# Score products over 64 rows instead of 32, other loads for their operands, and a new merge order

## Chip, cores and metric

One Trainium2 chip, one of its cores. The time is the device time of one execution in microseconds (us); lower is better. The kernel before takes 1289.83 us in the median of three runs.

## What is computed

The input `x` is 8 batches of 512 tokens by 128 features. Two blocks follow each other, both with a residual that is scaled by a gate per batch:

```python
h = layernorm(x) * (1 + ca) + sa
x = x + ga * global_attention(h)     # 16 heads of 8 channels over all 512 positions
h = layernorm(x) * (1 + cb) + sb
x = x + gb * local_attention_ffn(h)  # 2 layers: 8 heads of 64, windows of 64 tokens, then a gated MLP
```

The global attention, called A here, projects q, k and v (128 by 128 weights), regards them as 16 heads, and computes for each head

```python
attn = softmax(einsum('bhdt,bhds->bhts', k, v) * temperature)   # 512 x 512 for each of 16 heads
out  = einsum('bhdt,bhts->bhds', q, attn)
```

The contraction of the scores runs over only 8 channels. Each of k and v is split into a rounded high part and a low rest, and the four products of the parts are summed inside one matmul: 4 x 8 = 32 rows of contraction for a head.

## The kernel before

**Three streams.** For each engine the work is written as generators: stream `a` is the global attention of all 8 batches, stream `x` the local layers of the batches 0, 1, 2, 4, 6, stream `y` those of the batches 3, 5, 7. `merge` advances the generators in the order that a string names, one string per engine (`ORDER`, lines 65 to 117), one letter for a step. All engines execute their instructions in that fixed order and wait for each other by semaphores. `BANKS` (lines 118 to 130) gives the PSUM bank of every TensorE result in its order. Stream `y` shares memory with A, so it starts when A is through. So there are two phases: A with part of `x`, then `x` with `y`.

**Steps of A.** A batch has 16 groups (a group is 4 heads, one in each quarter q of the channels, at one quarter j of the 512 positions t), each group 2 steps (`half`) of 2 heads. A step: TensorE makes a pair of score products (`a_scores`, L436, 128 x 512 each, into two neighbouring banks); VectorE takes the maximum over both (`a_max`, L1151); ScalarE makes two exponentials with row sums (`a_exp`, L866). After two steps VectorE inverts the four sums, GpSimd scales q by them (L764), and TensorE adds the product with q for four heads (`a_values`, L445). The score pairs run two steps ahead of the exponentials. The next batch is prepared within the steps of the one before (normalization, transposition, projections, splitting into parts on GpSimd at L747 and L749).

**The path of k and v.** The parts go to DRAM (`k_scr`, `v_scr`, shape 4 quarters q x 4 heads hh x 4 parts x 8 channels x 512; L656) and come back as rows of 32 for a head: `v_rows` (two slots, for even and odd batches) and `k_rows` (one slot). A head of quarter q lies at 32 rows that rotate with hh, so a load for one hh takes one DMA of 4 quarters or two DMAs of 3 + 1, 2 + 2 or 1 + 3 quarters (`PIECES`, `rows_in`, L362): 7 DMAs for k and 7 for v in each batch. SP issues v first (`a_values_in`), then k for hh = 0 to 3 (`a_keys_in`), where the k of a hh waits until the batch before has used that slot; for batch 0 the v loads are issued by ScalarE. `a_scores` waits for v and k of its hh at the first step of each hh.

Of the kernel before, what the change touches and what calls it, by code (L numbers as in the profile page):

```python
# [48 lines left out]
PIECES = [[(q, n, (q + hh) % HQ) for q, n in ((0, HQ - hh), (HQ - hh, hh)) if n] for hh in range(HQ)]  # L49
# [44 lines left out]
    "ACT": (
        "aaaaaaaaaaaaaaaaaaaaaaaaaaaaaaaaaaaaaaaaaaaaaaaaaaxaaaaaaaaaaaaxxaaaxaaaxxaxxaaxxxaaxxxaxaaxaaaxxxxa"
        "xxxaaaxxaaaxaaxaaxaxxxxxaxxxaxxxaaaaaxaaxaaaaaxaaaaxaaxaaaxaaxaaxaxxaaxxxxxxxxxaxaaaxxxaxxaaaxaxaaax"
        "xaaaaaaxxaxaxaxxxaxxxxaaxxxaxaxaaaaaxaaaxaaaaaaaxaaaxaaaaaaaaaaaaaxaaaxaaxaxaxxxaxxaxxxaxxaxaxaaxxax"
        "xaaaxxaxxxaaaxxaxxxxaaaaxaaxxxaxaaxxaaxaaaaxxaaaaaxaaaaxaaaaxaaxaaaaaaaxaaaaaaaaaxxxxxxaaxxaxxxaxxxx"
        "xxaaxxxaxxaaaxxaxaaxxxxxaxxxaxxxaaxxaaaaaaaxaaaaxaaaaaaxxyyyxyyyxxyyyxxxxxxxxxxxxyyxyxxxxyyxxyxxxyxx"
        "xxxxyxxyyxxxyxyxxyyyyxxyyyxyyyyxyyxyyxyyyxyxxxxxxxxxxxxyxxxxyxxxxxyxxyxxxxxyxxxxxxxxyxxyyyxyyyyxyyxy"  # L100
        "yxyyyyyyyyxyyyxxyyxxyyyyyxxyxyyxyyxyxxxyxyyxxxxyxxxxxyxxxyxxxxxyxxxxxxxxxxyyxyyyxyyyyyyyxyyyxyyyyyxy"
        "yyxyyxxxxyxxyxxyxxxyyyxyyyyxxxyxyyxyxyxxyxxxyxxxxyxxyxxxxyxxyxxyyyyxyyyyxyyyxyxyyyyyyyyyyxyxxyxyxxyy"
        "xyyxyyxyxyyxxyxxyxxyyxxxxyxxxxyxxyxxxxxxxxxyxxxxxxyyxyyxyyyyyyxyyyyyxyyyyyxyyyxyyxyyyxxxxyyyxyyxyyyx"
        "yyyxxxyyxxxyxxxyxxxxyxyxxyxxxyxyyyyyyyyyyyxyyyyyxyxxyxyyyxxyyyyyyxyyxyyyyyyxyyxxyxyyy"
    ),
    "POOL": (
        "aaaaaaaaaaaaaaaaaaaaaaaaaaaaaaaaaxaxaxxaxaxxxxxaxxxaxxxaaaaxxaaxxxaxxaaaxaaaaaaaaaaaaxxxxxxxxxxaxxaa"
        "xxaxxaaaaaaxxaxaxxxaxaxaaaaaaaaaaaaaaaaaaaaaaxxxaxxxxxaxxxxaxxxaaxaaaxaxxaxaaxxaxxaaaaaaaaaaaaaaaaaa"
        "aaxxxaxaxxxxxxxxxxxxaaaaxxaxxxaxxaxaaaaaaaaaaayyyxxxxxxxxxxxxxxxxyyyyyyxxyxyxyyxyxyyxxyyyyyyyyxxxxxx"
        "xxxxxxxxxxxxxxxxxxyyyyyyyyyyyyyyyyyyxyyyxxyyxyxxxxxxxxxxxxxxxxxxxxyyyyyyyyyyyyyyyyxxxyxyxyxxyxxyxxyx"  # L110
        "xyxxyxxxxxxxxxyyyyyyyyyyyyyyyyyyxyxyyxyxyxyxxxxxxxxxxxxxxxxxxxyyyyyyyyyyyyyyyyxyyyxxyxyyyxyxxxxxxxxx"
        "xxxxxxyyyyyyyyyyyyxyyyyxxxyyyyyyyy"
    ),
    "SP": (
        "aaaaaaaaaaaaaaxaaaaaaaaaxaaaaaaaaaaaxaaxaaaaaaaaaaaaaxxxyxxyxyyxxyxyyxyxy"
# [22 lines left out]
def build(nc, x, wmod, wqkv1, wqkv, wo, w1, w2, cols_in, rows_in_, rotary, out):  # L138
    with ExitStack() as ctx:
# [503 lines left out]
        def _(sp):  # L643
# [776 lines left out]
```

## Time and profile before

| | |
|---|---|
| median of 3 runs | 1289.83 us (1284.92 to 1290.12) |
| the profiled execution | 1282.93 us, of which its span (first to last instruction) 1280.9 us |
| TensorE busy in the span | 1047.0 us (82%) |
| VectorE | 957.4 us (75%) |
| ScalarE | 920.6 us (72%) |
| GpSimd | 505.4 us (39%) |
| mean granted TensorE clock | 0.909 of full |

Engines: PE is TensorE's matmul, PEld its weight load, DVE VectorE, ACT ScalarE, POOL GpSimd, SP the engine that issues most DMAs. "Granted clock" is 1.00 for 2.4 GHz and 0.50 for 1.2 GHz, or a mean of the two over a stretch. A bracket with an arrow at the end of a timeline row is the idle time of the engine before the instruction and what ended it.

### The profile page before, as it was taken

Reading aid. Unit: us, or ns where it says so; the run is one execution under the profiler, and the core shown is the slowest. Engines: PE = TensorE matmul, PEld = TensorE weight load, DVE = VectorE, ACT = ScalarE, POOL = GpSimd, SP = SyncE. Lnnn points to the kernel's source line nnn. Section 1 sums busy time; section 2 is a strip of 40 time slices with the busy share of each in tenths; the row PEclk is TensorE's granted clock in tenths of the full one; section 3 lists DMA queues with packets and bytes.
Section 4 is the critical chain, followed back from the end, with each engine's and each line's share of the span. In section 5 each row is a group of like instructions: output and inputs, shape, how many; then the busy total and the mean of one; then the engine's idle time right before and its main releaser. Section 6 shows DMA issues by size and latency. Waiting matters only on the chain. (4 is left out here: it accounts for less than half of the span.)

```text
span 1280.9 us, 23838 instructions
## 1 busy us (share of the span) xinstructions
PE 1047.0 (82%) x8124; PEld 521.6 (41%) x8124; DVE 957.4 (75%) x1945; ACT 920.6 (72%) x2782; POOL 505.4 (39%) x577
## 2 busy tenths in 40 slices
PE   2677978788887888888887888898888987888887
PEld 1232334233432343234234545455355445445463
DVE  2669887788788979886788585885884777687745
ACT  1687969678997799969856757577577666676684
POOL 4111244033310631153039363564374356266550
PEclk7687869798996899879898999899999999999989
DMA  6331212103121040301001101011011011010010
GB/s 209 144 124 48 86 43 68 66 1 109 53 71 70 1 138 25 99 34 31 1 8 30 30 1 30 9 30 30 9 31 30 1 38 30 9 30 18 14 31 17
DMA packets 24647, 59.15 MB, mean 46 GB/s; under 512 B 2832, under 2 KB 3024, under 8 KB 23376
## 3 DMA queue, kind: packets, MB, share of 16 engines
q1 hardware_dynamic: 23394, 55.53, 14.4%
q10 hardware_dynamic: 1134, 2.10, 0.5%
q8 instruction: 67, 1.10, 0.4%
q14 instruction: 52, 0.43, 0.1%
HBM read 23.98 MB, written 18.87 MB: 33 GB/s over the span
## 5 line engine op out<-in xcount | busy, mean ns | idle before, releaser
L866 ACT ACTIVATE E<-psum,neg_max 128x512 f32<-128x512 f32 x512 | 347.9, 718 | 80.3 <-DVE neg_max L1151 56.5
L1151 DVE TENSOR_REDUCE neg_max<-psum 128x2 f32<-128x1024 f32 x256 | 307.8, 1214 | 75.3 <-PE psum L436 73.3
L786 POOL TENSOR_TENSOR work<-work,rot_work 128x512 f32<-128x512 f32 x128 | 162.6, 1271 | 154.2 <-DVE rot_work L1218 152.3
L436 PE MATMUL psum<-v_rows,k_rows 32*128 32x512 f32 x512 | 133.8, 557 | 100.9 <-ACT E L866 47.3
L799 POOL TENSOR_TENSOR rot_work<-rot_work,rz 128x512 f32<-128x512 f32 x128 | 132.8, 1039 | 206.3 <-DVE rz L1245 206.2
L960 ACT ACTIVATE rot_work<-psum,neg 128x128 f32<-128x128 f32 x512 | 184.5, 407 | 34.1 <-DVE neg L1240 26.2
L494 PE MATMUL psum<-wqkv_sb,hs 128*128 128x512 f32 x384 | 191.1, 633 | 7.3 <-DVE hs L1208 4.4
L764 POOL TENSOR_TENSOR qz<-qT,rz 128x32 f32<-128x32 f32 x128 | 30.8, 241 | 337.1 <-DVE rz L1155 337.0
L445 PE MATMUL psum<-E,qz 128*32 128x512 f32 x1024 | 162.2, 711 | 0.0
L436 PEld LDWEIGHTS psum<-v_rows,k_rows 32*128 32x128 f32 x512 | 52.9, 205 | 247.4 <-issue 122.3
L794 POOL TENSOR_TENSOR work<-work,rn 128x512 f32<-128x512 f32 x128 | 133.1, 1053 | 16.8 <-DVE rn L1110 16.6
L960 ACT ACTIVATION_READ_ACCUMULATOR rot_work<-psum,neg 128x1 f32 x512 | 124.6, 248 | 0.0
L866 ACT ACTIVATION_READ_ACCUMULATOR E<-psum,neg_max 128x1 f32 x512 | 121.7, 238 | 0.0
L501 PE MATMUL psum<-ident,work 128*128 128x128 f32 x512 | 88.8, 311 | 37.1 <-POOL work L794 22.8
L932 ACT ACTIVATE rot_work<-psum 128x512 f32<-128x512 f32 x128 | 76.9, 604 | 58.1 <-DVE ss L1222 35.2
L1240 DVE TENSOR_REDUCE neg<-psum 128x4 f32<-128x512 f32 x128 | 85.6, 678 | 40.2 <-PE psum L519 39.8
L494 PEld LDWEIGHTS psum<-wqkv_sb,hs 128*128 128x128 f32 x384 | 67.7, 197 | 93.4 <-issue 47.9
L1214 DVE TENSOR_TENSOR work<-psum,rot 128x512 f32<-128x512 f32 x128 | 87.2, 681 | 20.9 <-ACT rot_work L932 20.7
L569 PE MATMUL psum<-work,w_sb 128*128 128x512 f32 (+1 forms) x192 | 93.3, 610 | 11.4 <-ACT work L975 7.8
L529 PE MATMUL psum<-ident,rot_work 128*128 128x128 f32 x512 | 82.4, 287 | 22.5 <-POOL rot_work L799 12.5
L501 PEld LDWEIGHTS psum<-ident,work 128*128 128x128 f32 x512 | 63.5, 157 | 79.1 <-POOL work L794 53.8
L970 ACT ACTIVATE prT<-psum 128x512 f32<-128x512 f32 x128 | 81.1, 646 | 15.3 <-PE psum L540 12.3
(121 smaller groups left out, 1679.0 us busy)
## 6 DMA issues: line engine op xcount, KB each, us to landing
work<-v_al SPq DMA_DIRECT2D x16, 512.0 KB, 4.4
work<-v_al SPq DMA_DIRECT2D x16, 384.0 KB, 6.3
k_scr<-hi SPq DMA_DIRECT2D x16, 256.0 KB, 3.0
k_scr<-lo SPq DMA_DIRECT2D x16, 256.0 KB, 3.3
v_scr<-hi SPq DMA_DIRECT2D x14, 256.0 KB, 3.0
v_scr<-lo SPq DMA_DIRECT2D x14, 256.0 KB, 3.3
k_rows<-k_scr SPq DMA_DIRECT2D x16, 192.0 KB
v_rows<-v_scr SPq DMA_DIRECT2D x14, 192.0 KB
```

What stands on the lines that cost most here:

```text
L436: pe.matmul(bank, k_rows[r:r + 32, hh, P * j:P * (j + 1)], v_rows[r:r + 32, b % 2, hh, :], start=True, stop=True).then_inc(full, 1)
L445: last = pe.matmul(O_BANK[32 * q:32 * q + 32, :], qz[:, hh, j % QZ_SLOTS, q, :], E[:, (b * NG + g) % E_RING, q, :], start=(g == 0), stop=( ...
L494: pe.matmul(bank, hs[s][:, P * i:P * (i + 1)], wqkv_sb[:, l, INNER * c:INNER * (c + 1)], start=True, stop=True).then_inc(full, 1)
L501: last = pe.transpose(bank[:, P * p:P * (p + 1)], qk[s][:, i, w, P * p:P * (p + 1)], ident[:])
L569: pe.matmul(bank[0:CH[c]], w1_sb[:, l, o:o + CH[c]], h2T[s], start=True, stop=True).then_inc(full, 1)
L786: pool.tensor_tensor(qk[s][:, i, w, :], qk[s][:, i, w, :], sinp[s][:, n % 2, :], ALU.add).then_inc(rot_sum[s], 1)
L794: pool.tensor_tensor(v, v, rn[s][:, i, w, :].unsqueeze(2).broadcast_to([P, H, DH]), ALU.mult).then_inc((q_ready, k_ready)[w][s], 1)
L799: pool.tensor_tensor(pr[s][:, u % PR_SLOTS], pr[s][:, u % PR_SLOTS], rz2[s][:, u, :].unsqueeze(2).broadcast_to([P, 4, 2 * W]), ALU.mult).t ...
L866: act.activation(E[:, (b * NG + g) % E_RING, 2 * half + m, :], pair[:, m], ACT.Exp, bias=neg_max[:, n, m:m + 1], accum_out=z[:, n, m:m + 1 ...
L960: last = act.activation(pr[s][:, u % PR_SLOTS, w, :], bank[:, 2 * W * w:2 * W * (w + 1)], ACT.Exp, bias=neg2[s][:, u, w:w + 1], accum_out= ...
L1151: dve.tensor_reduce(neg_max[:, n, :], pair, AX.X, ALU.max, negate=True).then_inc(max_ready, 1)
L1214: dve.tensor_tensor(qk[s][:, i, w, :].rearrange("p (h d) -> p h d", h=H), bank.rearrange("p (h d) -> p h d", h=H), rot[:, l, i, w, 0, :].u ...
```

## The change

1. **Products over 64 rows.** A head of quarter q now lies at fixed rows: `GROUP_OF = [0, 2, 1, 3]`, so quarters 0 and 2 share the rows 0 to 63, quarters 1 and 3 the rows 64 to 127. `k_rows` becomes twice as large: slot 0 of its new axis holds the rows of the quarters 0 and 1, slot 1 those of 2 and 3, and all other rows are zero. A step multiplies 64 rows of `k_rows` with 64 rows of `v_rows`; the rows of the other head meet zeros. The two products of a step lie in the two halves of the rows.
2. **Zeros.** GpSimd sets all of `k_rows` (128 x 4096) to zero once at the start, and SP waits for it (`s_kzero`) ahead of the first k load.
3. **Loads.** v comes with two DMAs for each hh, each of two quarters (0 and 2, 1 and 3; 64 rows): 8 in a batch. k comes with four DMAs for each hh, each of one quarter (32 rows): 16 in a batch. The bytes are the same.
4. **New merge order.** All five strings of `ORDER`, and `BANKS`, are new. The steps of each stream are the same in number and kind.

```diff
-PIECES = [[(q, n, (q + hh) % HQ) for q, n in ((0, HQ - hh), (HQ - hh, hh)) if n] for hh in range(HQ)]
+GROUP_OF = [0, 2, 1, 3]
+V_PIECES = [(0, 2, 2), (1, 2, 2)]
+K_PIECES = [(q, 1, 1) for q in range(HQ)]
...
-            k_rows = sa("k_rows", [P, HQ, T], F32R)
+            k_rows = sa("k_rows", [P, 2, HQ, T], F32R)
...
-        def rows_landed(eng, s, b, hh):
-            passed(eng, s[hh], 16 * len(PIECES[hh]) * (b + 1))
-
-        def rows_in(eng, dst, scr, hh, landed):
-            for q, m, r in PIECES[hh]:
-                eng.dma_start(dst[32 * r:32 * (r + m)].bitcast(F32),
-                              scr[q:q + m, hh].rearrange("q t d s -> q (t d) s")).then_inc(landed[hh], 16)
+        def v_landed(eng, b, hh):
+            passed(eng, v_in[hh], 16 * len(V_PIECES) * (b + 1))
+
+        def k_landed(eng, b, hh):
+            passed(eng, k_in[hh], 16 * len(K_PIECES) * (b + 1))
+
+        def part_rows(scr, hh, q, step, m):
+            return scr[q:q + step * (m - 1) + 1:step, hh].rearrange("q t d s -> q (t d) s")
+
+        def values_in(eng, b, hh):
+            for q, step, m in V_PIECES:
+                r = 32 * GROUP_OF[q]
+                eng.dma_start(v_rows[r:r + 32 * m, b % 2, hh].bitcast(F32),
+                              part_rows(v_scr, hh, q, step, m)).then_inc(v_in[hh], 16)
+
+        def keys_in(eng, hh):
+            for q, step, m in K_PIECES:
+                r = 32 * GROUP_OF[q]
+                eng.dma_start(k_rows[r:r + 32 * m, q // 2, hh].bitcast(F32),
+                              part_rows(k_scr, hh, q, step, m)).then_inc(k_in[hh], 16)
...
                 for m, (bank, full) in enumerate(pair):
-                    r = 32 * ((2 * half + m + hh) % HQ)
-                    pe.matmul(bank, k_rows[r:r + 32, hh, P * j:P * (j + 1)], v_rows[r:r + 32, b % 2, hh, :],
+                    r = 2 * 32 * m
+                    pe.matmul(bank, k_rows[r:r + 64, half, hh, P * j:P * (j + 1)], v_rows[r:r + 64, b % 2, hh, :],
                               start=True, stop=True).then_inc(full, 1)
...
+                if b == 0 and hh == 0:
+                    sp.wait_ge(s_kzero, 1)
...
             pool.memset(clamp[:], SHIFT2).then_inc(s_clamp, 1)
+            pool.memset(k_rows[:].rearrange("p w q t -> p (w q t)").bitcast(F32), 0.0).then_inc(s_kzero, 1)
```

Of the order strings this is what the two have in common and what not. On each engine the last step of A stands behind nearly as many steps of `x` as before (TensorE 180 before and 186 after, VectorE 169 and 172, ScalarE 174 and 175, GpSimd 96 and 96, of 470, 435, 440 and 240). Between two events of A the number of `x` steps differs:

| steps of `x` on | batch 1 | 2 | 3 | 4 | 5 | 6 | 7 |
|---|---|---|---|---|---|---|---|
| TensorE, from the v projection of the batch to its first score pair, before | 0 | 11 | 6 | 13 | 8 | 12 | 8 |
| the same, after | 0 | 20 | 11 | 24 | 7 | 8 | 20 |
| VectorE, from the v split of the batch to the maximum of step 30 of the batch ahead of it, before | 0 | 4 | 5 | 9 | 5 | 17 | 3 |
| the same, after | 0 | 12 | 11 | 17 | 6 | 7 | 13 |

## Rows read from the trace of the kernel before

**Rows 1.** Stretches: length, busy us (x) of PE, PEld, DVE, ACT, POOL, clock, DMA, GB/s

```profile
37.10:640.00 602.90, 498.08 (x3294) 204.62 (x3295) 489.78 (x867) 496.05 (x1482) 171.76 (x260) 0.86 0.20 64
640.00:1281.00 641.00, 540.84 (x4797) 310.59 (x4795) 458.80 (x1046) 421.21 (x1295) 319.77 (x289) 0.97 0.09 21
```

**Rows 2.** Who waited for whom from 55.6 to 640: us, times, longest

```profile
DVE neg_max L1151 <- PE psum L436: 54.4, 68, 5.1
ACT E L866 <- DVE neg_max L1151: 30.2, 36, 2.6
...
PE psum L436 <- DMA k_rows<-k_scr: 9.8, 2, 7.0
```

**Rows 3.** The 17 low-clock stretches of that phase (first and sum), then the rest's sum

```profile
86.30:100.00 13.70, 9.04 (x36) 1.99 (x36) 6.58 (x15) 7.78 (x23) 0.72 (x3) 0.50 0.21 74
...
sum 150.10, PE 123.92 PEld 45.29 DVE 107.07 ACT 95.82 POOL 43.82; mean PE 7.29 PEld 2.66 DVE 6.30 ACT 5.64 POOL 2.58
...
sum 434.30, PE 361.31 PEld 155.36 DVE 367.86 ACT 387.11 POOL 127.22; mean PE 20.07 PEld 8.63 DVE 20.44 ACT 21.51 POOL 7.07
```

**Rows 4.** TensorE's L445 alone in the same low-clock stretches, sum

```profile
sum 150.10, PE 52.06; mean PE 3.06
```

**Rows 5.** Timeline of TensorE, 85 to 97: start, us, line, count, idle before

```profile
85.00 0.50 PE L436 MATMUL psum<-v_rows,k_rows 32*128 32x512 f32 x2
86.95 1.94 PE L445 MATMUL psum<-E,qz 128*32 128x512 f32 x8
94.26 0.79 PE L436 MATMUL psum<-v_rows,k_rows 32*128 32x512 f32 x2 [4.66 <-issue]
```

**Rows 6.** Timeline of TensorE, 233 to 245

```profile
233.78 0.51 PE L436 MATMUL psum<-v_rows,k_rows 32*128 32x512 f32 x4
234.22 1.07 PE L445 MATMUL psum<-E,qz 128*32 128x512 f32 x8
...
243.82 0.79 PE L436 MATMUL psum<-v_rows,k_rows 32*128 32x512 f32 x2 [7.01 <-DMA k_rows<-k_scr]
```

**Rows 7.** Four stretches, all engines

```profile
308.20:311.60 3.40, 2.33 (x14) 0.64 (x14) 2.67 (x4) 3.40 (x11) 0.24 (x1) 1.00 0.19 54
311.60:315.00 3.40, 3.22 (x14) 0.89 (x14) 2.28 (x3) 3.12 (x10) 0.24 (x1) 0.50 0.90 193
...
584.60:588.00 3.40, 1.99 (x14) 0.63 (x6) 3.15 (x6) 3.40 (x17) 2.04 (x2) 1.00 0.14 37
588.00:591.40 3.40, 2.62 (x30) 1.31 (x34) 1.96 (x4) 3.40 (x15) 1.28 (x2) 1.00 0.01 2
```

**Rows 8.** The first of these stretches, L436 alone

```profile
308.20:311.60 3.40, 1.40 (x6) 1.00 0.19 54
```

**Rows 9.** SP's timeline: first, third and last of seven loads of v

```profile
75.06 5.65 SPq L362 DMA_DIRECT2D v_rows<-v_scr  x7
...
224.56 5.57 SPq L362 DMA_DIRECT2D v_rows<-v_scr  x7
...
531.53 5.26 SPq L362 DMA_DIRECT2D v_rows<-v_scr  x7
```

**Rows 10.** L436 alone, how many products had started by a time

```profile
0.00:94.20 94.20, 17.82 (x64) 0.76 0.47 161
0.00:554.20 554.20, 116.86 (x449) 0.85 0.24 79
```

**Rows 11.** DMA in 40 slices of 148 to 163, GB/s

```profile
GB/s 98 104 98 98 93 71 76 76 71 82 71 175 120 71 76 76 55 49 49 49 49 55 49 49 49 49 55 49 49 126 126 44 76 66 55 49 71 82 71 76
```

**Rows 12.** Start, timelines of ScalarE and GpSimd

```profile
27.06 12.97 ACTq L362 DMA_DIRECT2D v_rows<-v_scr  x7
40.13 0.69 ACT L866 ACTIVATE E<-psum,neg_max 128x512 f32<-128x512 f32 x1 [25.54 <-DVE neg_max L1151]
...
4.30 0.94 POOL L742 MEMSET qz<- 128x1024 f32 x1
...
16.17 0.61 POOL L747 CAST hi<-kf 128x512 fp32r<-128x512 f32 x1 [10.87 <-DVEq L1147]
```

More of the change, by code:

```diff
@@ new lines @@
+        "xaaxaaaxaaaaaaaaxaaaaaxaaaaaxxxxaaxaxaaaaaaxaaaaaaaaaaaaaaaxaaxxaxaaxxxaxxxxaaaaxxaaxaaxxaaxaaaxaaxx"
+        "aaxaaaaaaaaxaaxaxaaxaaaaaaaaaaxxxxaaaxxxaaxaaaxxxaxaaaxaaaaaaxaaaaaaaaaxaaxaaxxaaaxxxaaaxaaaaaaxxxxx"
+        "xxxxxaaaxxaaaxaaxaaaxaxaaaxxaaaxxaaaaaaxxaaaxaaxaaaxxxaxaaaaaxaaaxxxaaaxxxaaaxaxaaaaaxaaaaxaxxxxxxaa"
+        "xxyyyxyyyyyyyyyyxxxxyxxyxxyyxxxyxyyyyyxyxyyyyxxyyxyyxyxxyyyxyxyxxxyxxxxyxyyyxxyyyxyxxyyxyxyyxyyyyyyy"
+        "xxxxxxyxyxyyxyxxxxyyyxxyxxxxyxyxyyyyxyyxyyyxxyyxyxyxyxxyxxxyxxyxxyyyyyxxxyxxyxxxyxyyyyyyyyxyyyxxxxxx"
@@ L92 @@
-        "yxyyyxxyxxxyyyyy"
+        "aaaaaaaaaaaaaaaaaaaaaaaaaaaaaaaaaaaaaaaaaaaaaaaaaaaaaaaaaaaaaaaaaaaxaaaaaaxaaaaaaaxaaaaaaaaaxaxxaaxx"
+        "axxaaxxaxaaxxaaaaaaxaaaaaaaaaaaaaaaaaaaaaaaaaaaaxxaxxxxaaaxaaaaaaaaaaxxaaxxxaaaxaxaaxxxaxaaxaaaaaaaa"
+        "xaaaxaaxaaaaxaaaxaaaaaaxxxaaaaaaxaxaaaxxxxaxxxxxxaaxaaxaaaaaaaxaaxxaxxaxxaaaxaaxxxxaxxxxxaaxxaaaaxaa"
+        "xaaaxxaaxaaaxaaaaaaaaaaaaaaaxxxaaxaaaaaaxaaaaaaxaaaaaxaaaaxaaaaxaxaaaaxxaaxaxxaxxaaxxaxaaaaaaaxaaaaa"
+        "aaaaxxaxxaxxaaxaaaaaaaaaaxxaxxaxaaaxxxxaxaaxaaaaaaxxaaxaxaaaxaaaxaaaaaaaaaaaaaxxxaaaxaxaaaaaxxxxaaax"
@@ new lines @@
+        "xaxxaaaxxaaaxaaxaaaaaxaaaaaaaaxxaxxxxaaaxaaaxxxxaxaaaaaxxaaaxxxaaaxxaaaxaaxaxaaaxaxaaaaaxxxayxyxxyxy"
+        "xyyyyyyyyyxyxyxxxxyxyyxyyxyyyxxxyyyyyyyyyyxyyxxyxxxxxyyxyxxxyxxxxxxyyyxyyxyxyxxxyxyyyyyxxyyxyxyxxxxy"
+        "xyyxxyyxyyxyxyyxyyyxyyxyyyyyyxyyxxyxxxxyxxxxxxxxyyyxxxyxxyyxyxxyxyxyyyyyyyxyxxyyxyxxxyxyyyyyyxyxxxyx"
+        "yyyyxxxyyxxyxyyxyyxxxyxxxxxyyxyxxxyxxxyxxxyyxyyxyyxyxxxyxyyyyyxxyxyyxxxxxxyxyyxyyyyyxxyyxyyyxyyxyyyx"
+        "yyxxxyxxxxxyyxyxxxyxxxxxyyxyxyxyyxyxxyxyxyyyyyyyyxxxyyxyxxxyxyyyyyyxyxxxxxyyxxxxyxyyyxyyyyyxyxxyxxxx"
@@ L93 @@
+        "xyyxyxxxxyxxxxxxyyyxyyxxxyxyxyyyyyyxxxyxyxyyxxxyxyxyxyyyyxxyyyxxyxyyyxyyyyyyxxxyxxxxxyyxyxxxxyxxxxxx"
+        "xxxxyyxyxyyxxxxx"
     ),
     "ACT": (
[L95 to L98, printed above, removed]
@@ new lines @@
+        "axxaxxaxxaaaaaaxxaxxxxaaaaxxxxaaaaxaaxxxaaxxaaaxaaaxaxaaxyyyxyyxyxyyyyyyyyyxxxyxxxyyyyyxxxyyxyxyxyyx"
+        "yyyyxxxyyxyyxyyxxyyxxyyxxxxyxxxxyxxyxyxxxyxxyyyxyyyxyyyxyyxyyyyyyxyxyxxxxyyyxxxxyxxyyxyyxyyyyxyyxxxy"
+        "yyxxyxyxxyxxyxxxxxyxxxxyxxxxxyyxyyxyyyyyyyxyyyyxyyyyyyyyxyyxxyyxyxxxxyyxxyxyxxxyyyxxyyxxyxxxyxyxxxyx"
+        "xxxyxxxyxxxyxyxxxyxxyyyyyxyyyxyyyxyxyyyyyyxyxxxxyyxxxxyxyyxyxyyyxxyyyyyyxxyyxxxyxxxxyxxxxyxxxyxxxyxy"
+        "xxxxxyyxyyxyyyyyyxyyyyyxyyyyyyyyxyyxxyyxyxxxxxxxxyyyxxxyyxxxyyyxxxyxyyxxxyyxxxxyxxxyxxxxyxxxyxxyxyyy"
@@ L105 @@
+        "yyxyyyyxyyxyyxyyyyxyxxxyyxyyxxxxyyxxyyyyxyxyxxyyyxxxyyyxxxyxyxxxxyxxxxyxxxxxxyxxyxxxx"
     ),
     "POOL": (
[L107 to L110, printed above, removed]
@@ L258, in build @@
         s_silexp, s_sil, s_setup = sem("s_silexp"), sem("s_sil"), sem("s_setup")
-        s_gcol, s_tables, s_clamp, s_qz = sem("s_gcol"), sem("s_tables"), sem("s_clamp"), sem("s_qz")
+        s_gcol, s_tables, s_clamp, s_qz, s_kzero = (
+            sem(n) for n in ("s_gcol", "s_tables", "s_clamp", "s_qz", "s_kzero"))
         s_chain = sem("s_chain")
```

86 lines of the change are left out of this document (36 added, 50 removed).

## The prediction, made before the changed kernel was run

> **What bounds the kernel now.** I first read the busy times by stretch. In A (37 to 640 us) VectorE and ScalarE are each busy some 0.82 and TensorE 0.83; in the second phase TensorE leads with 0.84 of 641 us [rows 1]. Nothing is saturated in A: the fixed order on five engines loses time in waits between them, in both directions, 54.4 us of VectorE for a score pair and 30.2 us of ScalarE for a maximum [rows 2]. The change touches A (products, loads) and, by the order alone, the second phase. So I ask what in A is lost to the clock and what to the loads.
>
> **The clock.** Between 80 and 640 us the granted clock is at its lower level (1.2 GHz) in 17 stretches of together 150.1 us. There ScalarE does 0.64 us of work in a us against 0.89 elsewhere, VectorE 0.71 against 0.85 [rows 3]. A score pair takes 0.79 us instead of 0.50 and the values of a group 1.94 instead of 1.07 [rows 5, 6]. So a group of A needs 2 x 0.79 + 1.94 = 3.52 us of TensorE, instead of 2 x 0.50 + 1.07 = 2.07. ScalarE needs four exponentials of 0.69 us, 2.76, for a group [rows 12]: at the upper level ScalarE sets the pace of pure A, at the lower one TensorE does, at 0.76 us more. The low stretches hold 52.06 / 1.94 = 27 groups [rows 4]: 20.4 us lost. The shares give a bracket: the same work at the pace of the rest takes 95.8 / 0.89 = 107.6 us by ScalarE and 126.4 by VectorE, of the 150.1; less about 10 us of them that are idle for a load (below), 32 and 14 us. I take 20.4.
>
> Does the changed product keep the clock up? At 308.2 TensorE was busy 2.33 of 3.40 us, with nothing but score pairs and values, and the clock fell behind that; at 584.6 it was busy only 1.99, with one pair and with products of `x`, and the clock stayed [rows 7, 8]. So the narrow pair seems to support the clock less than other work of the same length. A pair over 64 rows fills twice as much of the array in the same time, so I expect it to help; no row shows it. The Trainium skill (TensorE: Matmul & The Clock Gate, Part 1) ties the clock to how busy TensorE has been and says nothing of how many rows a product fills; by that, a pair of the same duration changes nothing, and the sum below would lose this term. The two rows above speak against so plain a rule; it is the second rival.
>
> Of the 150 us those stretches stay that follow a wait in which TensorE has no work: I count four waits for k (below) and four for chains of `x`, at some 5 us each, 40 us. So about 3/4 goes: **-15.5 us**, bounds 0 and -32. The first groups of batch 0 run at the lower level too; two of them may come at the upper one: **-1.5** (2 x 0.76).
>
> **The pair itself.** Two products in different quarters of the rows run side by side: two take 0.50 us, and four in a row, two steps, 0.51 [rows 5, 6]. The halves of a step stay side by side after the change, but two steps can't, since both want all rows. That costs up to the length of a pair beyond the first where two steps' pairs are neighbours in the timeline, some 28 times, say 0.2 us each; ScalarE and VectorE have the banks to work on then. 0, bound +6.
>
> **The zeros.** 128 x 1024 take 0.94 us, so 4096 take 3.8 us, on a GpSimd that is idle for 10.87 us until 16.17 [rows 12], where it begins to make the first parts of k; their load is later still. 0; without that cover 3.8.
>
> **The loads.** This speaks against the change. First products of a batch wait for its k of hh = 0. The 65th product, first of batch 1, starts at 94.26 [rows 5, 10], 19.2 us behind SP's first v issue at 75.06; the first of batch 3 at 243.82, 19.3 us behind 224.56 [rows 6, 9]. The trace names k's load for two waits, 9.8 us, 7.01 of it here; the other, 2.8, is that of batch 5 [rows 2]. TensorE waits 4.66, 7.01 and 2.8, 14.5 in all. The seven batches have such a load, the last begins at 531.53 and its first pair is out by 554.2, in time [rows 9, 10].
>
> Why 19.2 us for 1.25 MB? The rate falls in steps of about 25 GB/s: 98 to 104, then 71 to 76, at the end 49 GB/s, with single peaks of 126 to 175 [rows 11]. That fits loads that go by quarter: a DMA of 4, 3 or 2 quarters uses 4, 3 or 2 DMA engines with 64 KB each, always the same first ones, at 25 GB/s or 2.6 us; a DMA of one quarter is spread and gives the peaks. Ahead of k of hh = 0 stand five v DMAs of several quarters, and it is one itself: 6 x 2.6 = 15.6, and 3.6 for the rest (start, landing, two single quarters). After the change eight v DMAs of two quarters, all on the same two engines, take 20.8; four spread k DMAs behind them some 0.7; with 3.6 this is 25.1. So **k of hh = 0 lands 5.9 us later** though its own DMAs are quicker. k of the other hh lands right behind and is not late. The skill's page DMA: Bandwidth & Descriptors (Why a DMA increments its semaphore by 16 and not by 1) says it so: the slowest dimension of both sides sets how many engines a DMA uses, lowest-numbered first. The trace agrees with its steps of 25 GB/s.
>
> Which batches would wait? The new order decides, by the steps of `x` in that stretch. Batch 1 has none, as before: 4.7 + 5.9 = 10.6 us. Batch 5 has 7 for 8: 8.7. Batch 6 did not wait, but now has 4 fewer on TensorE and 10 fewer on VectorE while k comes 5.9 later: I take 5. Batch 3 has 5 to 6 more steps of some 1 us, which covers it: about 7. Batches 2, 4 and 7 have 8 to 12 more and wait for nothing. In all 31 instead of 14.5. Behind the waiting pair all of TensorE's queue stands, `x` too; VectorE and ScalarE eat up what is ready for 0.5 to 2 us of each. **+15 us**, bounds -12 (the steps of `x` cover all) and +35 (all seven wait 5.9 more).
>
> At the start the v loads stand in ScalarE's queue: 12.97 us for 7 issues, until 40.0, and the first exponential follows at 40.13 [rows 12]. Eight issues with as many bytes for each of the first two engines but without k's load beside them: 0, bounds -3 and +3. SP issues 24 instead of 14 loads a batch, 10 x 0.65 us, in a queue that waits most of the time: 0.
>
> **The order.** Both orders put nearly the same work of `x` under A (TensorE 186 steps for 180), so the second phase, with the same steps and no score pair, is only mixed otherwise. 0, with 8 us either way: no row prices it.
>
> **The sum**: -15.5 - 1.5 + 15 = -2, on the profiled 1282.93: 1281. The median of the runs stands 1.0054 above the profiled one: 1288; I say 1287, the clock being the less well bounded and the wider term.
>
> **Rivals.**
> 1. *Clock gains, loads cancel* (the forecast): 1287, own range 1277 to 1298. Chance 0.38.
> 2. *The clock doesn't answer to rows.* Only the loads remain: +15, and +22 if each wait drags a low stretch behind it: 1305. It ends slower, and decides as soon as less than 9 us come from the clock while batches 1, 5, 3 and 6 wait over 30 us in all. For it: pairs last as long as before. Against: [rows 7]. Chance 0.22.
> 3. *The clock gains and the steps of `x` cover the loads*: only batch 1 and 5 wait, 19 for 14.5, and 20 us come from the clock: 1282.9 - 17 = 1266, median scale 1273; down to 1255. For it: 20 and 24 steps of `x` before the first pairs of batches 2 and 4. Chance 0.27.
> 4. *The new order fits worse in the second phase*, which is half of the time and bound by TensorE: +12, 1299. Nothing for or against. Chance 0.13.
>
> **Numbers.** 1287. Range 1262 to 1308: it leaves out 0.1 on each side, of rival 3 and of rival 2. A half per cent, 6.4 us, is about what a measurement tells here. Faster (below 1283.4): 0.25 of rival 3 and 0.13 of the forecast, 0.38. Slower (above 1296.3): rival 2 0.2, rival 4 0.08, forecast 0.06, 0.34. The rest 0.28.
>
> **What would show it.** Right: pairs of 0.50 us with 64 x 128 forms; in A a granted clock over 0.92 for 0.86; the first pair of batch 1 some 25 us behind SP's first v issue, with a wait near 10 us; 49 GB/s in the v load; the second phase at 641 us within 8. Wrong: waits at k under 15 us in all (loads or order), a clock in A of 0.86 or lower, pairs of 0.7 us (not side by side), or a second phase off by 10 us.

## The result and the profile after

The changed kernel takes **1298.69 us** in the median of 14 runs (1290.84 to 1301.72), the kernel before 1287.96 (1284.52 to 1291.97, 14 runs) beside it: a ratio of **1.0076**, 95% interval 1.0062 to 1.0090. It is slower by 9.8 us (0.0076 x 1288). The forecast was 1287 and leaned to faster; the time lies inside the range of 1262 to 1308, but the change went the other way. Ratios here and below leave out one execution of a later version (v by quarters), which took 5106 us where its others took 1252 to 1257.

The two phases, by stretches of the changed kernel (length; busy us and count of PE, PEld, DVE, ACT, POOL; clock; DMA share; GB/s). The first runs from the first score pair to the last residual of A:

```profile
40.90:668.20 627.30, 491.88 (x3309) 204.81 (x3310) 484.55 (x870) 500.59 (x1486) 172.56 (x260) 0.88 0.20 61
668.20:1298.00 629.80, 535.04 (x4782) 313.38 (x4780) 454.69 (x1043) 416.33 (x1290) 317.49 (x288) 0.95 0.09 22
```

Beside [rows 1]: A starts 3.8 us later and takes 627.3 us (before: 604.2, from 37.1 to the same event at 641.3), and the second phase takes 629.8 instead of 639.6. The engines do the same amount of work in A, TensorE even 6 us less, at a clock of 0.88 for 0.86. So A's 23 us are waiting. Once A is under way, the timeline of TensorE has four waits of more than 5 us in it, all before the first pair of a batch (start, us, idle before it):

```profile
104.15 0.80 PE L454 MATMUL psum<-v_rows,k_rows 64*128 64x512 f32 x2 [11.97 <-DMA k_rows<-k_scr]
...
248.34 0.80 PE L454 MATMUL psum<-v_rows,k_rows 64*128 64x512 f32 x2 [5.59 <-issue]
...
417.02 0.79 PE L454 MATMUL psum<-v_rows,k_rows 64*128 64x512 f32 x2 [9.58 <-DMA k_rows<-k_scr]
...
504.06 0.79 PE L454 MATMUL psum<-v_rows,k_rows 64*128 64x512 f32 x2 [7.34 <-DMA k_rows<-k_scr]
```

They are the waits for k, 34.5 us in all; [rows 5, 6] have two of the three of the kernel before, which come to 14.5. For the second one the trace names no load (`issue`), as for the 4.66 us of [rows 5]; that it is k's too is read from its place, 25.8 us behind the v issue like the others, and from its going with other loads (below). SP's timeline has the v loads ahead of them:

```profile
78.65 12.64 SPq L374 DMA_DIRECT2D v_rows<-v_scr  x8
...
222.54 13.23 SPq L374 DMA_DIRECT2D v_rows<-v_scr  x8
...
391.15 12.34 SPq L374 DMA_DIRECT2D v_rows<-v_scr  x8
478.39 12.65 SPq L374 DMA_DIRECT2D v_rows<-v_scr  x8
```

The first pair follows the first v issue by 25.5, 25.8, 25.9 and 25.7 us (before 19.2 and 19.3). SP itself takes 12.3 to 13.2 us to issue 8 of them, where [rows 9] have 5.3 to 5.7 for 7. The rate while they run, 40 slices from 78 to 104:

```profile
DMA  1000111111121111111111111475565755646111
GB/s 44 0 0 9 25 32 50 54 50 50 50 88 50 50 50 54 50 54 50 50 50 50 50 50 50 139 183 164 158 170 164 173 183 148 195 123 173 44 47 50
```

50 GB/s at a DMA share of 0.1: that is what two engines of 16 would carry, at the prediction's 25 GB/s for one, and k runs only from 94 on. At the start the same loads stand in ScalarE's queue:

```profile
30.94 14.29 ACTq L374 DMA_DIRECT2D v_rows<-v_scr  x8
...
45.33 0.69 ACT L887 ACTIVATE E<-psum,neg_max 128x512 f32<-128x512 f32 x1 [27.30 <-issue]
```

The first exponential is 5.2 us later than in [rows 12]. Part of that comes from something I had priced at nothing, the zeros (timelines of VectorE and of GpSimd, the latter's last row):

```profile
4.59 4.19 DVE L1094 TENSOR_SCALAR cT<-cT 128x8 f32<-128x8 f32 x1 [4.59 <-ACT cT L861]
8.82 0.20 DVE L1095 RECIPROCAL cT<-cT 128x8 f32<-128x8 f32 x1
...
5.25 3.50 POOL L764 MEMSET k_rows<- 128x4096 f32 x1
```

The same instruction of VectorE took 0.38 us in the kernel before:

```profile
4.96 0.38 DVE L1073 TENSOR_SCALAR cT<-cT 128x8 f32<-128x8 f32 x1 [4.96 <-ACT cT L840]
```

Even these 0.38 us are not its length alone: it ends at 5.34, just behind GpSimd's earlier write of 128 x 1024 (4.30 to 5.24, [rows 12]), and in a version where GpSimd writes nothing beside it (zeros on VectorE, below) it takes 0.11. In the changed kernel it ends with GpSimd's write of the zeros (8.78 and 8.75), TensorE's first product starts at 9.37 instead of 5.92, and all of the start is 3.5 us later. GpSimd had nothing to do then, as the prediction said; what was not free is VectorE beside it. The Trainium skill (SBUF — State Buffer, Who interferes with whom) has this: a VectorE copy or `tensor_scalar` in a two-port mode shares a pair of ports with GpSimd, and who comes second is blocked for the other's whole instruction. The trace agrees in the main, 4.19 us for 0.38; but VectorE stood waiting from 4.59, behind the earlier write, and the write of the zeros, which began at 5.25, still went ahead of it.

Last, the stretches of A at the lower clock, from 61 us on (first and second of 19, and their sum):

```profile
95.80:109.40 13.60, 5.25 (x22) 1.22 (x22) 3.02 (x7) 1.93 (x5) 0.24 (x1) 0.50 0.30 88
119.70:123.10 3.40, 3.40 (x16) 1.16 (x15) 3.00 (x14) 2.37 (x7) 0.24 (x1) 0.50 0.00 0
...
sum 133.20, PE 95.41 PEld 36.86 DVE 77.01 ACT 76.20 POOL 36.75; mean PE 5.02 PEld 1.94 DVE 4.05 ACT 4.01 POOL 1.93
```

133 us for 150 [rows 3], and four of them (from 95.8, 246.0, 406.4 and 498.6 on; 47.7 us together) lie around the four waits.

### The profile page after: what moved, and what is told of

It reads as the page before. It is cut to its first block, busy times and chain, and to the rows that moved or that the text cites. A ratio compares the mean times of both kernels' runs of the same rounds, so it can differ in the third digit from the quotient of the medians.

```text
span 1298.0 us, 23922 instructions
## 1 busy us (share of the span) xinstructions
PE 1036.2 (80%) x8124; PEld 525.7 (40%) x8124; DVE 951.9 (73%) x1945; ACT 920.3 (71%) x2782; POOL 507.4 (39%) x578
## 4 chain that ended last, share of the span: by engine, by line
PE 28%; DVE 23%; ACT 9%; POOL 5%; issue 4%; SPq 3%; DMA 2%; DVEq 0%; ACTq 0%; POOLq 0%
PE psum L512 4%; PE psum L568 4%; DVE neg_max L1172 4%; PE psum L587 4%; PE psum L558 4%; ACT rot_work L981 3%; DVE rot_work L1239 3%; DVE ss L1243 3%; DVE work L1235 3%; POOL work L815 2%; PE psum L537 2%; PE psum L463 2%; PE psum L547 2%; SPq L374 2%; ACT E L887 2%
## 5 line engine op out<-in xcount | busy, mean ns | idle before, releaser
L454 PE MATMUL psum<-v_rows,k_rows 64*128 64x512 f32 x512 | 136.3, 536 | 125.2 <-ACT E L887 55.5
L454 PEld LDWEIGHTS psum<-v_rows,k_rows 64*128 64x128 f32 x512 | 54.0, 203 | 272.1 <-issue 158.5
L463 PE MATMUL psum<-E,qz 128*32 128x512 f32 x1024 | 156.4, 687 | 0.0
L815 POOL TENSOR_TENSOR work<-work,rn 128x512 f32<-128x512 f32 x128 | 133.2, 1053 | 19.5 <-DVE rn L1131 19.2
L981 ACT ACTIVATION_READ_ACCUMULATOR rot_work<-psum,neg 128x1 f32 x512 | 117.6, 230 | 0.0
L887 ACT ACTIVATION_READ_ACCUMULATOR E<-psum,neg_max 128x1 f32 x512 | 113.6, 222 | 0.0
L547 PE MATMUL psum<-ident,rot_work 128*128 128x128 f32 x512 | 83.8, 290 | 31.1 <-POOL rot_work L820 26.9
L1261 DVE TENSOR_REDUCE neg<-psum 128x4 f32<-128x512 f32 x128 | 85.4, 677 | 29.1 <-PE psum L537 28.9
```

The lines of the kernel that those rows point to most:

```text
L454: pe.matmul(bank, k_rows[r:r + 64, half, hh, P * j:P * (j + 1)], v_rows[r:r + 64, b % 2, hh, :], start=True, stop=True).then_inc(full, 1)
L463: last = pe.matmul(O_BANK[32 * q:32 * q + 32, :], qz[:, hh, j % QZ_SLOTS, q, :], E[:, (b * NG + g) % E_RING, q, :], start=(g == 0), stop=( ...
L815: pool.tensor_tensor(v, v, rn[s][:, i, w, :].unsqueeze(2).broadcast_to([P, H, DH]), ALU.mult).then_inc((q_ready, k_ready)[w][s], 1)
L887: act.activation(E[:, (b * NG + g) % E_RING, 2 * half + m, :], pair[:, m], ACT.Exp, bias=neg_max[:, n, m:m + 1], accum_out=z[:, n, m:m + 1 ...
L981: last = act.activation(pr[s][:, u % PR_SLOTS, w, :], bank[:, 2 * W * w:2 * W * (w + 1)], ACT.Exp, bias=neg2[s][:, u, w:w + 1], accum_out= ...
```

## The experiments

Ratios are to the kernel before beside which each ran (1286.91 to 1289.02 us in the median); a difference of two ratios is turned into us with 1288. "Waits for k" is TensorE's idle time before the first pairs of the batches 1 to 7, where it is over 1 us, whatever the trace names for it. "A" and "second phase" are cut as above; "lower clock in A" leaves out the first 20 us of A. These last four columns are of one profiled execution each, the first two of all.

| kernel | median us | ratio, 95% | waits for k | A | second phase | lower clock in A |
|---|---|---|---|---|---|---|
| before | 1288 | 1 | 14.5 | 604.2 | 639.6 | 150.2 |
| changed | 1298.69 | 1.0076 (1.0062 to 1.0090) | 34.5 | 627.3 | 629.8 | 133.1 |
| v by quarters | 1255.55 | 0.9752 (0.9727 to 0.9777) | 0 | 588.3 | 631.0 | 85.3 |
| 32-row products | 1307.87 | 1.0163 (1.0139 to 1.0188) | 27.9 | 634.9 | 631.4 | 187.7 |
| changed, old order | 1320.68 | 1.0267 (1.0242 to 1.0292) | 52.6 | 635.7 | 642.4 | 126.3 |
| before, new order | 1278.47 | 0.9941 (0.9917 to 0.9964) | 6.9 | 611.1 | 627.4 | 163.8 |
| before, loads by quarters | 1269.97 | 0.9869 (0.9838 to 0.9900) | 0 | 595.2 | 640.6 | 139.9 |
| v by quarters, 32 rows | 1265.88 | 0.9826 (0.9795 to 0.9857) | 0 | 601.3 | 627.4 | 150.2 |
| v by quarters, old order | 1257.55 | 0.9767 (0.9736 to 0.9799) | 0 | 580.1 | 642.3 | 78.5 |
| before, new order, loads by quarters | 1263.20 | 0.9826 (0.9798 to 0.9854) | 0 | 603.8 | 631.3 | 157.0 |
| k first | 1264.19 | 0.9800 (0.9782 to 0.9818) | 0 | 588.9 | 627.8 | 81.9 |

### The loads by themselves: v by quarters

```diff
-V_PIECES = [(0, 2, 2), (1, 2, 2)]
+V_PIECES = [(q, 1, 1) for q in range(HQ)]
```

> The changed kernel, but v is loaded like k, one quarter to a DMA (16 DMAs of 32 rows for a batch instead of 8 of 64). Theory L, the loads: the changed kernel waits 11.97, 5.59, 9.58 and 7.34 us for the first k of batches 1, 3, 5 and 6, because eight two-quarter DMAs of v stand ahead of it on two DMA engines. Then the four waits all but vanish (under 2 us each) and the time falls by 25 to 40 us against the changed kernel, to about 1265. Theory O, the order: the new merge order itself costs the time, the waits are only where it shows; then the waits move to other producers and the time stays within 8 us of 1298. Theory R, the rows: the 64-row products cost it; the time stays as well.

1255.55 us, ratio 0.9752 (0.9727 to 0.9777): with sixteen small DMAs for eight larger ones the kernel is 41.7 us faster than as changed (1.0076 - 0.9752). The profile is that of one more execution of the same kernel:

> The changed kernel with single-quarter loads of v once more, for its profile: the four waits for k under 2 us each, the first k of a batch some 13 us behind SP's first v issue (32 issues of 0.65 us, of which 20 until then), and the low clock of A at under 110 us.

1256.58 us. Its rows of SP and ScalarE:

```profile
72.80 7.54 SPq L374 DMA_DIRECT2D v_rows<-v_scr  x16
...
38.33 0.69 ACT L887 ACTIVATE E<-psum,neg_max 128x512 f32<-128x512 f32 x1 [20.28 <-DVE neg_max L1172]
```

16 issues take 7.54 us, the 8 took 12.64; no pair waits for k, and the first exponential comes 7.0 us earlier. And the sum of its 12 stretches at the lower clock, 85.4 us for 133.2:

```profile
sum 85.40, PE 73.19 PEld 29.12 DVE 61.88 ACT 61.09 POOL 40.24; mean PE 6.10 PEld 2.43 DVE 5.16 ACT 5.09 POOL 3.35
```

The loads are the largest term of the change. Of the recorded theories, L holds, with a fall just above the 25 to 40 us that it gave.

### What stands ahead, or how the DMAs are cut? k first

The eight v loads stay as they are; only SP's step with k of hh = 0 moves ahead of them.

```diff
                     for n in range(2):
                         a_parts(b, n)
                         yield
+                    a_keys_in(b, 0)
+                    yield
                     a_values_in(b)
                     yield
-                    for hh in range(HQ):
+                    for hh in range(1, HQ):
                         a_keys_in(b, hh)
                         yield
```

> The changed kernel with one step of SP's queue moved: from batch 1 on, the k load of hh = 0 is issued before the eight v loads instead of behind them. Sizes, count and shape of all loads stay. Theory 1 (k waits because it stands behind eight two-quarter loads on the same two DMA engines): the waits of 11.97, 5.59, 9.58 and 7.34 us before the first pairs of batches 1, 3, 5 and 6 go, for v of hh = 0 is then only two loads behind; the first pair lands some 9 us behind the first v issue instead of 25.5 to 25.9, and with 34.5 us of waits gone and the start unchanged (first exponential at 45.3) the median is 1260 to 1268. Theory 2 (two-quarter loads are slow by their number and shape wherever they stand, and later products then wait for v of hh = 1 to 3): first pairs come early, but the waits turn up again before the later score steps, and the time stays above 1285.

1264.19 us (1259.94 to 1264.79), ratio 0.9800 (0.9782 to 0.9818): 35.6 us faster than the changed kernel, as theory 1 said. SP's issues are as slow as ever, and the first pair of batch 1 waits for an exponential, not for a load:

```profile
80.98 12.44 SPq L374 DMA_DIRECT2D v_rows<-v_scr  x8
```

```profile
94.94 0.50 PE L454 MATMUL psum<-v_rows,k_rows 64*128 64x512 f32 x2 [0.75 <-ACT E L889]
```

So slow v loads cost nothing as such: what cost was that the first k stood behind them. The 6 us to the version with v by quarters would fit the start, where the first exponential is still at 45.64 instead of 38.33. The pair came 14.0 us behind the first v issue, not the 9 I had written; by then nothing waited for the load, so this is no longer a landing time.

### The order and the loads of the kernel before

> The changed kernel (64 rows, new loads, zeros) with the merge order and banks of the kernel before. Theory L: k of hh = 0 lands 25.5 us behind SP's first v issue here too, and the old order has fewer steps of x in that stretch, so it waits more, in batches 1 to 7, some 45 us in all, and the time is 1305 to 1318. Theory O, the new order is what made it slower: the time falls to 1280 to 1290. The second phase tells the order's worth by itself: 641 us with the old order, 630 with the new.

> The kernel before (32 rows, old loads) with the new merge order and banks. Theory L with an order that is as good or better: k of hh = 0 lands 19.3 us behind the first v issue again; the waits come to 12 to 16 us, the second phase to 630, and the time to about 1275 to 1282. Theory O: the time is 1295 or more.

> The kernel before (32 rows, its order) with all loads of k and v cut into single quarters, 32 DMAs for a batch instead of 14. Theory L: its three waits for k, 14.5 us, go, and the clock with them a little: 1262 to 1274. If the number of DMAs mattered more than the engines that they use, it would not get faster than 1285.

> Single-quarter loads, 64 rows, the old order. With the slow loads the new order was worth 22 us (1320.7 against 1298.7), at the old loads 8.5. Theory: 22 was 8 to 10 of the order itself and the rest steps of x in front of the first k of a batch; with loads that no one waits for only 5 to 10 us are left: 1261 to 1266.

> The kernel before with the new order and with k and v loads of one quarter each: no zeros, 32-row products, k beside one another instead of in two windows. Beside the changed kernel with v of one quarter and 32-row products (1265.9, which has the zeros and the new layout) it gives what zeros and layout cost together, with loads out of the way. Theory 1 (only the zeros, 3.5 us): 1262 to 1263. Theory 2 (the layout costs or helps by itself; old order gave 1270.0, the order alone -8.5): 1261.5 if the order's gain carries over whole.

In the kernel before, loads by quarters are one line:

```diff
-PIECES = [[(q, n, (q + hh) % HQ) for q, n in ((0, HQ - hh), (HQ - hh, hh)) if n] for hh in range(HQ)]
+PIECES = [[(q, 1, (q + hh) % HQ) for q in range(HQ)] for hh in range(HQ)]
```

**Order.** Alone on the kernel before the new order gives 0.9941: -7.6 us. The time is as theory L said; the waits for k are not, 6.9 us (before the batches 1 and 5) for its 12 to 16. Its phases in the stretches view (compare [rows 1]):

```profile
37.90:649.00 611.10, 507.96 (x3310) 209.13 (x3310) 484.52 (x870) 502.69 (x1486) 172.74 (x260) 0.85 0.20 63
649.00:1276.00 627.00, 528.83 (x4782) 309.15 (x4780) 454.56 (x1043) 416.56 (x1290) 317.69 (x288) 0.97 0.09 22
```

Cut at the same event, the second phase is 12.6 us shorter with 11 us less TensorE time in it (539.5 to 528.8), and A 7 us longer, though it waits 7.6 us less for k. Beside the slow loads the new order is worth far more, 1.0267 - 1.0076 = 24.6 us. The old one waits 52.6 us for k there, before all seven batches, against 34.5; the trace names k's load for six of the waits (us, times, longest):

```profile
PE psum L454 <- DMA k_rows<-k_scr: 48.7, 6, 12.7
```

With loads by quarters it is worth 0.9767 - 0.9752 = 1.9 us with 64 rows and 0.9869 - 0.9826 = 5.5 us with 32, intervals of some -3 to 7 and 0 to 11. The recorded theory had 5 to 10 us for the first of these. So most of what the order gives beside the slow loads is that it puts steps of `x` where k is late.

The last kernel of the five, at 1263.20 us (0.9826), beside v by quarters with 32 rows (0.9826; this is the second kernel under the next heading), leaves nothing to be seen of zeros and layout together, within some 5 us.

**Loads.** Five pairs of kernels differ only in their loads, all by quarters in one of them. "Start" is how much earlier the first exponential comes with quarters.

| the kernel's loads against quarters | gain of quarters, us | waits for k that go | start |
|---|---|---|---|
| before | 16.9 | 14.5 | 4.5 |
| before, new order | 14.8 | 6.9 | 5.4 |
| changed | 41.7 | 34.5 | 7.0 |
| changed, 32-row products | 43.4 | 27.9 | 7.4 |
| changed, old order | 64.4 | 52.6 | 6.7 |

What the prediction calls its loads' term is what the loads cost in the changed kernel less what they cost in the kernel before, each with its own order: 41.7 - 16.9 = 24.8 us (interval some 19 to 30), with 20.0 us more of waits and 2.5 of start. With one order on both sides it is more: 26.9 or 28.6 with the new one (64 or 32 rows), 47.5 with the old. How much a late load costs depends on the order that stands around it. Waits and start together come to within 3 us of the gain in the first three lines, and 8 and 5 us short of it in the last two, with intervals of some 4 to 5 us: a us of wait costs about a us of time, or a little more.

### The 64 rows by themselves

The layout, the loads and the zeros stay; each product takes only its own 32 rows.

```diff
-                    r = 2 * 32 * m
-                    pe.matmul(bank, k_rows[r:r + 64, half, hh, P * j:P * (j + 1)], v_rows[r:r + 64, b % 2, hh, :],
+                    r = 32 * GROUP_OF[2 * half + m]
+                    pe.matmul(bank, k_rows[r:r + 32, half, hh, P * j:P * (j + 1)], v_rows[r:r + 32, b % 2, hh, :],
```

> The changed kernel with its loads, layout and order, but each score product over its own 32 rows only. Theory C, the clock answers to the rows: without the 64 rows the low-clock stretches of A grow from about 133 to 160 us or more, and the time rises by 8 to 20 us against the changed kernel. Rival N, the rows do nothing: the granted clock in A stays at 0.88 within 0.01 and the time within 4 us of the changed kernel's 1298. Rival S, the wide products cost something themselves (neighbouring steps no longer side by side): it gets faster by 3 to 8 us.

> Single-quarter loads of v and k, the new order, but products over 32 rows. With the 64 rows this came to 1255.5. Theory C: the rows give back some 9 us as they did beside the slow loads (1307.9 against 1298.7), so 1262 to 1268; more, if the waits for k hid a part of it. Rival: the gain of the rows came only from rising faster behind the waits, and is below 3 us here: 1255 to 1259.

1307.87 and 1265.88 us. Beside slow loads the 64 rows are worth 1.0163 - 1.0076 = 11.2 us (interval some 8 to 15), with loads by quarters 0.9826 - 0.9752 = 9.5 us (some 4 to 15). The pair has the same length with either number of rows (0.50 and 0.79 us at the two levels); what differs is the granted clock. With v by quarters, A with 64 rows and with 32:

```profile
35.30:623.60 588.30, 483.98 (x3309) 202.57 (x3310) 483.75 (x870) 500.48 (x1486) 172.81 (x260) 0.91 0.22 65
...
35.00:636.30 601.30, 505.32 (x3309) 207.63 (x3310) 484.73 (x870) 501.13 (x1486) 172.65 (x260) 0.86 0.22 64
```

TensorE was busy 0.82 of the time with 64 rows and 0.84 with 32, so it isn't by being busier that the wide products keep the clock. With 32 rows and v by quarters, the sum of the stretches at the lower clock is

```profile
sum 150.10, PE 131.94 PEld 49.09 DVE 111.26 ACT 113.22 POOL 44.63; mean PE 8.80 PEld 3.27 DVE 7.42 ACT 7.55 POOL 2.98
```

150.1 us for 85.4 with 64 rows, the same kernel otherwise; beside slow loads 187.7 for 133.1, and with the old order and quarter loads 139.9 for 78.5 (there with layout and zeros). In each pair, products of unchanged length that fill more rows leave 55 to 65 us less at 1.2 GHz. These sums are of one profile each, and they scatter: 64-row kernels with fast loads that differ only in their start have 61 to 85 us, and the changed kernel with its zeros on VectorE has 112.6 for 133.1. But the mean clock is on record for every execution, and (but for the one of 5106 us) the two ranges of a pair never overlap: 0.930 to 0.940 with 64 rows against 0.907 to 0.916 (v by quarters), 0.914 to 0.927 against 0.891 to 0.896 (as changed), 0.939 to 0.948 against 0.906 to 0.914 (old order). Rival 2 falls. The 32 rows that a product gained hold zeros in `k_rows` and another head's parts in `v_rows`; whether it matters what they hold was not tried.

### The zeros

> The kernel before, with one instruction more: GpSimd writes 128 x 4000 zeros (beside the 4096 of the changed kernel) into a tensor that nothing reads, at the place of the changed kernel's zeros. Nothing waits for it by a semaphore. Theory 1 (GpSimd's write holds VectorE up at 4.6 us): the TENSOR_SCALAR of cT takes about 4.1 instead of 0.38 us, the start is 3.4 us later, and the median 1290 to 1293, +2.5 to +3.5. Theory 2 (the start is lengthened by something else in the changed kernel, or the delay is covered by the loads behind it): same as before, within 1 us.

```diff
+            pad_zero = sa("pad_zero", [P, 4000], F32)
...
             pool.memset(clamp[:], SHIFT2).then_inc(s_clamp, 1)
+            pool.memset(pad_zero[:], 0.0)
```

1293.23 us (12 runs) beside 1287.99 (17 runs): ratio 1.0032 (1.0015 to 1.0049), +4.1 us (1.9 to 6.3). VectorE's and GpSimd's rows, in a kernel in which nothing waits for this write:

```profile
4.55 4.16 DVE L1075 TENSOR_SCALAR cT<-cT 128x8 f32<-128x8 f32 x1 [4.55 <-ACT cT L842]
...
5.25 3.42 POOL L745 MEMSET pad_zero<- 128x4000 f32 x1
```

> The changed kernel with the zeros of k_rows written by VectorE as its first instruction, before ScalarE hands it anything (4.6 us), instead of by GpSimd at 5.25. Theory 1 (GpSimd's write of 3.50 us kept VectorE's next instruction waiting, and all of the start with it): that instruction takes 0.4 us again instead of 4.19; VectorE's own write of 4096 elements goes at 0.94 to 1.06 ns an element (work, 512 elements in 485 ns), 3.9 to 4.3 us, so it ends about as ScalarE's first result comes; the first product is at 5.9 to 6.3 us instead of 9.37, everything of the start 3 to 3.5 us earlier, the median 1295 to 1296. Theory 2 (the 3.5 us at the start are covered by the v loads in ScalarE's queue): the first exponential stays at 45.3 and the median at 1298 to 1299.

```diff
+            dve.memset(k_rows[:].rearrange("p w q t -> p (w q t)").bitcast(F32), 0.0).then_inc(s_kzero, 1)
             s_start(0)
...
-            pool.memset(k_rows[:].rearrange("p w q t -> p (w q t)").bitcast(F32), 0.0).then_inc(s_kzero, 1)
```

1297.82 us, ratio 1.0065 (1.0052 to 1.0078): 1.4 us below the changed kernel by the ratios, with intervals that overlap, so no gain is shown and the 1295 to 1296 of theory 1 is missed. VectorE's write started at 3.33, not at the beginning, and took 3.47 us, so it is in the way too and the start is 2.0 us earlier, not 3 to 3.5; the first exponential moves from 45.33 to 43.59.

### Together, and the best version

> The changed kernel with v loads of one quarter each and the zeros written by VectorE first. If the two terms add up: 1255.6 less 3 to 3.5 us, 1252, first exponential at 35 instead of 38.33. If the start is covered by something else, 1255.5.

> As the previous one, and for batch 0 SP issues v of hh = 0 between k of hh = 0 and k of the other hh, ScalarE only v of hh = 1 to 3 (12 issues instead of 16). Theory 1: the first pair waits for v of hh = 0 to land behind 1 MB of k; it then comes about 2 us earlier and ScalarE's queue is free 1.9 us earlier, so the time is 1.5 to 2 us below the previous one, 1250. Theory 2: ScalarE's exponentials follow the first maxima only, and k of hh = 1 to 3 then lands later and makes the second quarter wait: same as the previous one within 1 us.

> The version with v of one quarter and v of hh = 0 issued by SP at the start, with the zeros on GpSimd again but only once VectorE has finished the modulation (it then has nothing to do for about 4 us while TensorE makes k), instead of as VectorE's first instruction. If the zeros now hide entirely, the first product is at 5.9 us (7.41 with the zeros on VectorE), the first score pair 1.5 us earlier, and the median 1.5 to 2 us below 1250.0, so 1248 to 1248.5; if GpSimd's write then delays the split of k (it needs GpSimd at 16 us), 1250 or more.

```diff
             a_parts(0, 0)
-            for hh in range(HQ):
-                a_keys_in(0, hh)
+            a_keys_in(0, 0)
+            passed(sp, v_out, 16 * 4)
+            values_in(sp, 0, 0)
+            for hh in range(1, HQ):
+                a_keys_in(0, hh)
...
             pool.memset(clamp[:], SHIFT2).then_inc(s_clamp, 1)
+            pool.wait_ge(s_setup, 1)
             pool.memset(k_rows[:].rearrange("p w q t -> p (w q t)").bitcast(F32), 0.0).then_inc(s_kzero, 1)
```

1250.52 (ratio 0.9706, 0.9687 to 0.9725), 1250.02 (0.9688, 0.9667 to 0.9708) and 1250.24 us (0.9698, 0.9675 to 0.9721). The first is below v by quarters alone (0.9752); the three don't differ from each other, so neither of the 1.5 to 2 us that the last two were to bring is seen. In the last the zeros hold nothing up: VectorE's instruction takes 0.72 us (it still waits for the end of GpSimd's earlier write at 5.24), the first product starts at 5.92 as in the kernel before, GpSimd writes the zeros from 10.87 to 14.38, while VectorE waits for TensorE, and is idle for 2.20 us behind them:

```profile
4.62 0.72 DVE L1098 TENSOR_SCALAR cT<-cT 128x8 f32<-128x8 f32 x1 [4.62 <-ACT cT L865]
...
10.87 3.51 POOL L768 MEMSET k_rows<- 128x4096 f32 x1 [5.56 <-DVE rows L1112]
```

Its first exponential is at 33.67, against 35.18 of the version before it, but its A takes 588.4 us against 585.0: 1.5 us gained at the start are no longer there at the end. Why is open: its profile is of its slowest execution (1254.99 us), and the two kernels' profiles differ by 14 us in their time at the lower clock. Any of the three is 3% faster than the kernel before and 3.7% faster than the changed one.

## Why the prediction was wrong

The sum of the prediction, beside what the runs give for each term (ratios times 1288):

| term | predicted | measured |
|---|---|---|
| 64 rows (clock, with the start) | -17 | -9.5 with fast loads; -11.2 beside the loads of the change |
| loads | +15 | +24.8 |
| pair, SP's issues | 0 | not seen |
| zeros | 0 (3.8 without cover) | 0 with layout beside fast loads, 5 either way; +4.1 alone |
| order | 0 (8 either way) | -5.5 with fast loads and 32 rows; -7.6 alone |
| sum of the first figures | -2 | +9.8 |

The first figures of the last column add up to the change's +9.8 by construction: they are the steps of one path from kernel to kernel (quarter loads in the kernel before, then the order, zeros and layout, the 64 rows, and the loads of the change). On other paths the terms are other ones, up to -24.6 for the order. The sum of the prediction was 12 us off: 10 by the loads and 7.5 by the clock, both in the same direction, less 5.5 by the order, for which it had 0. That the time came as near as it did is in part luck.

**What failed is the size of the loads' term**: the +15 of the sum measured +24.8. The clock's term failed beside it: -17 measured -9.5 to -11.2.

*The loads.* The mechanism stood, nearly to the number: k of hh = 0 lands 25.1 us behind the first v issue (25.5 to 25.9), the batches that wait are 1, 3, 5 and 6, with 10.6, 7, 8.7 and 5 us predicted and 11.97, 5.59, 9.58 and 7.34 measured, 34.5 for 31. The Trainium skill (DMA: Bandwidth & Descriptors, Why a DMA increments its semaphore by 16 and not by 1) was right on how many engines such a DMA uses: 50 GB/s for v throughout. What was off is the size, in three parts. The waits grew by 20.0 us, not 16.5. The sum took a us of wait as a little less than a us of time (16.5 as 15), where the five pairs above give about one us or a little more. The start: v in ScalarE's queue costs the first exponential 7.0 us (45.33 against 38.33), where loads by quarters in the kernel before gain 4.5 (40.13 against 35.65); I gave 0, bound +3, and it is 2.5. These three make 7.5 of the 10 us; the rest is inside the noise of the term. Whether the clock is in it was not measured by itself. It does answer to the waits: v by quarters takes 47.8 us of lower clock out of A (133.1 to 85.3), in the kernel before 10.3 (150.2 to 139.9). A slow stretch behind each wait was in rival 2 (+22 instead of +15) and not in the forecast; its price stays open.

*The clock.* The direction, which only [rows 7, 8] spoke for, was right: the clock answers to rows, and the term that would have been struck out by the Trainium skill (TensorE: Matmul & The Clock Gate, Part 1) is there. That part speaks only of how busy TensorE is; these runs show that this isn't all, with TensorE busy 0.82 of A with 64 rows and 0.84 with 32. The step "about 3/4 goes" was too much: 64 rows take away 43% of the lower clock with fast loads (150.2 to 85.3) and 29% beside the loads of the change (187.7 to 133.1). I had assumed that all but the stretches behind waits were owed to the narrow pair; the 12 stretches that are left with 64 rows and no wait for k show that they weren't. Clock in A: 0.88, predicted over 0.92.

*The zeros.* "On a GpSimd that is idle" named the wrong cover. The question was who else can't work meanwhile. The bound of 3.8 us was right (3.5 measured for the write), and in the kernel before it was due in full, +4.1; in the changed kernel, where slow loads stand behind the start, it isn't shown (1.4 us when VectorE writes them, inside the noise).

*The order.* The 0 was a guess between bounds, and -7.6 lies at one end. The second phase went from 639.6 to 629.8 us, outside the 641 within 8 that I had named as the sign of being right. Rival 4 had the term, with the wrong sign. And the term isn't one number: beside the slow loads it is -24.6. Order and loads have no price apart from each other.

*Rivals.* Rival 3 needed the steps of `x` to cover the k of batches 3 and 6; they didn't (5.59 and 7.34). Rival 2's own threshold, under 9 us from the clock with over 30 us of waits, was missed by little: 34.5 us of waits, but 9.5 to 11 from the clock. The time fell between it and the forecast.

## What to carry to other kernels

A DMA over part of the rows can be slow through its cut; look at what stands ahead of the first transfer that somebody waits for, and move that one forward (35.6 us here without changing a DMA) before changing sizes. Measure parts of a change apart, and beside more than one setting of the others: here 64 rows and the order each gain, the loads lose more than both, and the version with v by quarters instead is 3.2% faster than the whole. An engine being idle is no cover for work that blocks a neighbour: ask what the neighbour is about to do.

## What the runs showed of the hardware

- The granted clock answers to how many rows products fill, at unchanged product times and with TensorE busy 0.82 against 0.84 of the time: 85.3 us of A at the lower level with 64 rows, 150.2 with 32, same order, same loads; over all executions a mean clock of 0.930 to 0.940 against 0.907 to 0.916.
- GpSimd's write of 128 x 4096 (3.50 us) held a VectorE `tensor_scalar` over 128 x 8 for 4.19 us instead of 0.38 (0.11 with no write beside it), though VectorE's instruction had started 0.66 us before the write; the same write 5.6 us later, when VectorE had nothing to do, held nothing.
- Issuing 8 DMAs of 128 KB, which moved 50 GB/s together, took SP 12.6 us, 16 of 64 KB with the same bytes 7.5 us. What takes SP the time per issue no run shows by itself.
